# First expert layer of a fused two-layer kernel: a space of its own for every quad's weights, and another order of the matmuls

## The reference, cut to what matters

```python
xn = _layernorm(x)
x = x + _L0_attn_ref(xn, ...) + _L0_ffn_ref(xn, ...)   # causal attention, 8 heads; mixture of 14 experts
xn = _layernorm(x)
x = x + _L1_attn_ref(xn, ...) + _L1_ffn_ref(xn, ...)   # selective scan, 16 states; 8 experts, 2 per row

def _L0_ffn_ref(h, router_w, w1, b1, w2, b2):
    logits = x @ router_w
    assignments = jnp.argmax(logits, axis=-1)
    probs = jax.nn.softmax(logits, axis=-1)
    weights = jnp.take_along_axis(probs, assignments[:, None], axis=1)[:, 0]
    hid = jax.nn.gelu(jnp.einsum('nd,edf->nef', x, w1) + b1, approximate=False)
    all_out = jnp.einsum('nef,efd->ned', hid, w2) + b2
    sel = jnp.take_along_axis(all_out, assignments[:, None, None], axis=1)[:, 0, :]
    return sel * weights[:, None]
```

## Time and profile before

| what | value |
|---|---|
| time, median of 3 runs | 797.71 us (796.41 to 802.4) |
| the profiled execution's own time | 792.92 us |
| its span in the profile | 791.0 us |
| TensorE busy | 669.5 us, 85% |
| VectorE busy | 542.7 us, 69% |
| ScalarE busy | 400.5 us, 51% |
| the expert stage in the trace | 240.4 to 279.0 us |

### The profile page before, as it was taken

How to read it: one execution, slowest core, us unless ns; L and a number is a source line. 1 busy time by engine, 2 the same in 40 slices (tenths; PEclk the granted TensorE clock), 3 DMA queues, 4 the chain that set the end, 5 groups by cost and what they waited for, 6 DMA issues and landing times. The chain is left out here.

```text
span 791.0 us, 11454 instructions
## 1 busy us (share of the span) xinstructions
PE 669.5 (85%) x3446; PEld 462.2 (58%) x3447; DVE 542.7 (69%) x846; ACT 400.5 (51%) x810; POOL 227.0 (29%) x179
## 2 busy tenths in 40 slices
PE   3889999999989907879899998997787999977664
PEld 2666777777758804345566555554637988862222
DVE  6184444444332222499999999999794678997998
ACT  1246565655524503846765566555556566662330
POOL 0012122112200051002022212224036136668881
PEclk9589999999998966899999999999898999997998
DMA  8400000000336920214666767677734455521112
GB/s 287 147 3 11 11 11 10 7 7 7 113 120 192 313 63 17 63 54 116 164 165 157 182 150 174 148 182 184 238 77 131 146 177 159 172 69 37 27 33 60
DMA packets 59803, 86.74 MB, mean 110 GB/s; under 512 B 7505, under 2 KB 35922, under 8 KB 59762
## 3 DMA queue, kind: packets, MB, share of 16 engines
q1 hardware_dynamic: 41330, 57.89, 23.2%
q0 software_dynamic: 7680, 23.08, 13.5%
q10 hardware_dynamic: 10752, 5.24, 2.2%
HBM read 54.60 MB, written 14.81 MB: 88 GB/s over the span
## 5 line engine op out<-in xcount | busy, mean ns | idle before, releaser
L1538 DVE TENSOR_REDUCE nmax<-PS 128x1 f32<-128x128 f32 (+7 forms) x128 | 95.8, 748 | 90.3 <-PE PS L979 90.2
L1007 PE MATMUL PS<-ROOM 128*128 128x512 f32 (+3 forms) x384 | 142.5, 489 | 0.5 <-ACT ROOM L661 0.5
L668 ACT ACTIVATE ROOM<-PS,nmax 128x128 f32<-128x128 f32 (+7 forms) x128 | 95.7, 748 | 76.8 <-DVE nmax L1538 75.0
L661 ACT COPY ROOM<-PS 128x512 f32<-128x512 f32 (+1 forms) x192 | 85.8, 484 | 77.1 <-PE PS L991 76.9
L991 PE MATMUL PS<-CST,ROOM 128*128 128x128 f32 x576 | 85.7, 276 | 10.5 <-ACT ROOM L661 10.5
L542 POOL DMA_DIRECT2D ROOM<-ROOM x32 | 28.6, 893 | 214.9 <-DVE ROOM L1622 212.8
L991 PEld LDWEIGHTS PS<-CST,ROOM 128*128 128x128 f32 x576 | 64.3, 142 | 38.6 <-issue 28.1
L976 PE MATMUL PS<-LATER 128*128 128x512 f32 (+2 forms) x192 | 77.1, 511 | 8.1 <-ACT ROOM L668 5.8
L1007 PEld LDWEIGHTS PS<-ROOM 128*128 128x128 f32 x384 | 64.9, 191 | 28.3 <-issue 25.1
L1614 DVE TENSOR_TENSOR_SCAN ROOM<-ROOM 128x1024 f32<-128x1024 f32 x32 | 72.7, 2271 | 0.5 <-ACT ROOM L700 0.2
L507 POOL DMA_INDIRECT rows_in<-XN,slot x48 | 62.8, 1309 | 20.0 <-issue 12.4
(11 more groups left out here) (176 smaller groups left out, 1230.4 us busy)
## 6 DMA issues: line engine op xcount, KB each, us to landing
ROOM<-bc_rows SPq DMA_DIRECT2D x32, 512.0 KB, 4.1
ROOM<-ROOM POOLq DMA_DIRECT2D x32, 512.0 KB, 6.1
LATER<-in_w SPq DMA_DIRECT2D x48, 256.0 KB, 3.0
ROOM<-in_w SPq DMA_DIRECT2D x32, 321.0 KB, 3.9
rows_in<-zero SPq DMA_DIRECT2D x20, 256.0 KB, 3.2
LATER<-rows_in SPq DMA_DIRECT2D x24, 128.0 KB, 2.8
rows_out<-ROOM ACTq DMA_DIRECT2D x24, 128.0 KB, 2.0
ROOM<-rows_in SPq DMA_DIRECT2D x8, 256.0 KB, 4.1
```

The source lines that it names most:

```text
L661: nc.scalar.copy(dst, src).then_inc(s_ed, 1)
L668: nc.scalar.activation(PR[:, s, 0:nk], sc[:, 0:nk], ACT.Exp, bias=nmax[:, i % 4:i % 4 + 1], accum_out=rsum[:, i:i + 1]).then_inc(s_ex, 1)
L1007: r = mm(PS[:, 6, lo:BANK], V[:, j, :], PT[:, 4 * group + j, lo:BANK], start=j == 0, stop=True, skip_group_check=True)
L1538: nc.vector.tensor_reduce(nmax[:, i % 4:i % 4 + 1], sc[:, 0:(i + 1) * P], AX_X, ALU.max, negate=True).then_inc(s_nm, 1)
```

## The change

It gives every quad its own space for weights. Six of the eight are loaded as soon as the experts of the tiles are known and the queue gets there, which is during the first attention; the spaces of quads 6 and 7 still lie over `PT`. The GELU's results have two sets of buffers (`MH2`), and the hidden units' PSUM banks are 2 and 3 for even quads and 5 and 6 for odd ones. The loops of one pass are written out. The order on TensorE becomes turn(p), hidden(p), result(p-1). VectorE's order stays as it was.

```diff
-        W4 = (mw0[:, 0:4, :], mw0[:, 4:8, :], more_w, more_w2)
-        X4 = (MX[:, 0:4, :], MX[:, 4:8, :], more_x, more_x2)
+        quad_w = 4 * W_ROW[0]
+        W8 = [room(HEAD_END + i * quad_w, [4, W_ROW[0]]) for i in range(6)]
+        W8 += [room(29 * KB + i * quad_w, [4, W_ROW[0]]) for i in range(2)]
+        moe_at = HEAD_END + 6 * quad_w
+        MXT = room(moe_at, [8, P])
+        MH2 = (room(moe_at + 4 * KB, [8, P]), room(16 * KB, [8, P]))
+        MY = room(moe_at + 8 * KB, [8, D])
+        X4 = [room(moe_at + (12 + 2 * i) * KB, [4, D]) for i in range(3)] + [room(50 * KB, [4, D])]
...
+        HIDDEN_BANK = (2, 5)
...
             def first_expert_loads():
                 e_n = MOE[0][0]
                 sp.wait_ge(s_eid, 1)
+
+                def rows(p):
+                    if p >= 4:
+                        sp.wait_ge(s_mtp[0], p - 3)
+                    sp.dma_start(X4[p % 4], xs[0][p * 4 * P:(p + 1) * 4 * P, :].rearrange("(i p) d -> p i d", p=P)
+                                 ).then_inc(s_mx[0][p % 4], 16)
+
+                def weights(p):
+                    for i in range(4):
+                        e = sp.value_load(eid[0][0:1, 4 * p + i:4 * p + i + 1], min_val=0, max_val=e_n - 1)
+                        sp.dma_start(W8[p][:, i, :], A["w_0"][bass.ds(e, 1)].rearrange("o p n -> (o p) n")
+                                     ).then_inc(s_mw[p % 4], 16)
+
+                for p in range(6):
+                    weights(p)
                 sp.wait_ge(s_sc[0], 16 * NT)
...
+                for p in range(3):
+                    rows(p)
+                sp.wait_ge(s_we, 2 * HEADS)
+                rows(3)
+                weights(6)
+                weights(7)
+                for p in range(4, QUADS):
+                    rows(p)
...
                 turn_rows(0, 0, 1, True)
                 hidden(0, 0, 1)
                 turn_rows(1, 1, 1, True)
-                result(0, 0, True)
+                pe.wait_ge(s_ke, 4)
+                pe.wait_ge(s_ve, 4)
                 hidden(1, 1, 1)
-                for s in (2, 3):
-                    turn_rows(s, s, 1)
-                    result(s - 1, s - 1)
-                    hidden(s, s, 1)
-                with pe.Fori(1, QUADS // 4) as r:
-                    for s in range(4):
-                        turn_rows(4 * r + s, s, r + 1)
-                        result(4 * r + s - 1, (s - 1) % 4)
-                        hidden(4 * r + s, s, r + 1)
-                result(QUADS - 1, 3)
+                result(0, True)
+                for p in range(2, QUADS):
+                    turn_rows(p, p % 4, p // 4 + 1)
+                    hidden(p, p % 4, p // 4 + 1)
+                    result(p - 1)
+                result(QUADS - 1)
                 pe.wait_ge(s_my[0], QUADS)
...
             experts_first()
-            pe.wait_ge(s_ke, 4)
-            pe.wait_ge(s_ve, 4)
             transposes(2)
```

More of the change, by code:

```diff
@@ L133, in build @@
         KB = 256
-        HEAD_END, MOE_END, END = 53 * KB, 90 * KB, 133 * KB
+        HEAD_END, END = 53 * KB, 133 * KB
         ROOM = sb("ROOM", [P, END])
@@ L427, in first_expert_loads @@
                 sp.wait_ge(s_eid, 1)
-                sp.wait_ge(s_sc[0], 16 * NT)
[L430 to L443, removed]
-                for s in range(4):
[L446 to L449, removed]
+                def rows(p):
[10 more added lines that the diff above has]
+                    weights(p)
+                sp.wait_ge(s_sc[0], 16 * NT)
+                for p in range(3):
[6 more added lines that the diff above has]
+                    rows(p)
             def second_expert_loads():
@@ L726, in experts_first, with quad @@
             def experts_first():
-                def quad(p, s):
+                def quad(p):
                     for i in range(4):
@@ L731, in quad @@
                                 act.wait_ge(s_mhp[0], 2 * p + i // 2 + 1)
-                            w = W4[s][:, i, 4 * P:4 * P + 2]
-                            r = nc.scalar.activation(MH[:, 2 * i + c, :], PS[:, 2 + i // 2, (2 * (i % 2) + c) * P:(2 * (i % 2) + c + 1) * P],
+                            w = W8[p][:, i, 4 * P:4 * P + 2]
+                            r = nc.scalar.activation(MH2[p % 2][:, 2 * i + c, :], PS[:, HIDDEN_BANK[p % 2] + i // 2, (2 * (i % 2) + c) * P:(2 * (i % 2) + c + 1) * P],
                                                      ACT.Gelu, bias=w[:, c:c + 1])
@@ L740, in store @@
                                   ).then_inc(s_mo[0][s], 16)
[L743 to L750, removed]
+                quad(0)
+                for p in range(1, QUADS):
+                    quad(p)
+                    store(p - 1, (p - 1) % 2)
                 store(QUADS - 1, 1)
@@ L1114, in hidden, with result @@
                         for c in range(2):
-                            r = mm(PS[:, 2 + i // 2, (2 * (i % 2) + c) * P:(2 * (i % 2) + c + 1) * P],
-                                   W4[s][:, i, c * P:(c + 1) * P], MXT[:, 4 * (s % 2) + i, :], start=True, stop=True)
+                            r = mm(PS[:, HIDDEN_BANK[p % 2] + i // 2, (2 * (i % 2) + c) * P:(2 * (i % 2) + c + 1) * P],
+                                   W8[p][:, i, c * P:(c + 1) * P], MXT[:, 4 * (s % 2) + i, :], start=True, stop=True)
                         if i % 2:
                             r.then_inc(s_mhp[0], 1)
-                def result(p, s, first=False):
+                def result(p, first=False):
                     if not first:
@@ L1656, in rows, with result @@
                     cp(MXT[:, 4 * s:4 * s + 4, :], bank(s).rearrange("p (i n) -> p i n", n=P)).then_inc(s_mt[0], 1)
-                def result(p, w, s, times):
+                def result(p, s, times):
                     dve.wait_ge(s_myp[0], p + 1)
@@ L1663, in result @@
                     tt(MY[:, 4 * s:4 * s + 4, :], bank(4).rearrange("p (i n) -> p i n", n=P),
-                       W4[w][:, :, 4 * P + 2:4 * P + 2 + D], ALU.add).then_inc(s_my[0], 1)
+                       W8[p][:, :, 4 * P + 2:4 * P + 2 + D], ALU.add).then_inc(s_my[0], 1)
                 rows(0, 0)
[L1667 to L1682, removed]
+                for p in range(1, QUADS):
+                    rows(p, p % 2)
+                    result(p - 1, (p - 1) % 2, (p - 1) // 2 if p > 2 else None)
+                result(QUADS - 1, 1, QUADS // 2 - 1)
             def combine_first(b):
```

13 lines of the change are left out of this document (1 added, 12 removed).

## The result

The changed kernel took 809.6 us (median of 6 runs, 802.18 to 812.13) beside 799.57 us for the kernel before (6 runs, 791.17 to 803.47, the three of the table above among them). The ratio is 1.0135, 95% interval 1.0092 to 1.0178. Ratios here are of fast runs alone, without those more than 1.5% above the fastest of their kernel (here the 803.47), and so they are not the quotients of the medians. I had forecast +7.0 us, 0.9%, as a change within one per cent. It is slower by more than that in this comparison: 0.0135 of 797.71 is 10.8 us, and the two medians differ by 10.0. The time itself lies inside the range that I gave, 801.5 to 810.

The account below looks back on a forecast made before the run. TensorE was taken to bound the expert stage's steady quads, at 4.01 us each. Added 1.05 + 7.3 + 1.05 = 9.4 us, less 2.4 removed, gave +7.0 on 797.71: 804.7 us, 0.9% more, range 801.5 to 810.

Parts of the forecast that it names:

- Where the stage stands: Expert stage before GpSimd's first gather: it is exposed, so a microsecond there is a microsecond of the kernel.
- The waits for weights: TensorE's waits for late weights at quads 6 and 7 go: 2.09 us removed.
- The GELU: Between hidden and result: it never holds result up in steady quads, so two sets of its buffers bring nothing.
- the 0.3 us at the end: From quad 7's hidden to the last addition: 0.29 us read as waits for the last GELU, to be removed.
- The uncovered copy: Between turn and hidden: VectorE's copy of turned rows leaves gaps of 1.22 us in quads 2 to 7, 1.05 in quad 1.
- The end: Before the last result group: it waits 1.05 us for the addition of quad 6, as both results use bank 4.
- The sum: Whole expert stage: 9.4 us added less 2.4 removed, +7.0 us.
- The loads beside the attention: 24 weight transfers during the first attention, from about 155 to 179 us: cost zero, bounds zero to +2 us.
- The clock: TensorE in the expert stage: granted clock from 246 to 285 us not under 0.95, else the prediction is wrong.
- a rival with 14%: Expert stage: TensorE's clock falls one to three times among the gaps, 2.6 to 7.8 us more, about 809; chance 14%.
- How the numbers follow: Last step, whole kernel: forecast 76%, 22 points above the one per cent line; within 1% 0.58, slower 0.40, faster 0.02.

Follow-up runs that it names:

- e2: The changed kernel with the old order on TensorE (turn, result, hidden), all else of the change kept; 796.1 us beside 797.55, ratio 0.9993.
- e5: The changed kernel with VectorE's copy of quad p+1 put ahead of its addition of quad p-1; one run, 805.26 us.
- e6: The changed kernel with the results in PSUM banks 4 and 7 by turns; one run, 805.35 us.
- e1: The changed kernel measured again without edit; 805.63 us beside 797.55 for the kernel before, ratio 1.0098.
- e3: The changed kernel with all weight transfers moved back behind the wait for the scatters; 804.26 us beside 797.55, ratio 1.0087.
- e7: The changed kernel with four useless matmuls per quad between turn and hidden of quads 1 to 7; 804.63 us beside 799.82, ratio 1.0076.
- e10: The changed kernel measured a third time without edit; 813.4 us beside 806.25 for the kernel before, ratio 1.0080.

## Why the prediction was right in its sum and wrong in its call

- *Where the stage stands.* Right: from the last addition on everything moved with it, with 0.12 us more to the gather.
- *The waits for weights.* Right: gone, 2.08 us by e2 against 2.09.
- *The GELU.* Right: no quad waits for it, and the 0.3 us at the end belongs to the old order (e2).
- *The uncovered copy.* Right: 1.21 against 1.22, and both of its parts by e5: 1.05 for the trip over VectorE, and the rest for the addition in its way.
- *The end.* Right: 1.05 us, and e6 takes it away.
- *The sum.* +7.0 for the stage. Apart from the first, the traces of this order (e1, e3, e7, e10) had stages of 44.61 to 45.53 us against 44.93. Five comparisons of kernels with this order have ratios of 1.0135, 1.0098, 1.0080, 1.0087 and 1.0076; 7.0 us is 1.0088.
- *The loads beside the attention.* Right at zero: 0.2 us in the first trace, nothing that shows over all of them. The queue took 25.9 us to issue the 24, not 24.4, and was done at 181.5 to 184.6 and not at 179, still long before the scatters.
- *The clock.* Wrong by my own mark. I had asked for a granted clock of at least 0.95 from 246 to 285; it was 0.84 there in the first trace, 0.50 until 258.
- **The term of the sum that failed is the clock at the stage's start.** The sum took the start of the stage over from the one trace of the kernel before, as if the clock came back at the same time, and left a later return to a rival with 14%. Against the 44.93 of the sum the three traces of the changed kernel had +2.5, -0.15 and +0.6 us, and where more was needed it was the clock's late return after turn of quad 0. Their mean is 45.9, 7.9 above the mean of the two traces of the kernel before; the three comparisons together have 7.7, and the sum had 7.0. The rival priced this well, 2.6 us for one fall, but as a new fall among the gaps. What came was a late return from a fall ahead of the stage, which e2, with the old order, showed too, by 1 us. I count it to the spread of the executions, which is not shown.
- **The step that turned this into a wrong call is the last one, "How the numbers follow".** The forecast stood 1.0 us below the line of one per cent, and I called it "within 1%" with 0.58, with 22 of its 76 points above the line. The 7 us come on top of a time that differs by some 10 us from run to run, so a measurement could fall on either side of the line. The microsecond that the clock adds on the mean of the three traces would have put the sum at the line itself, and the chances at even. The direction was never in doubt, and on which side of the line a comparison fell was in part chance: of the three, two are below it.

Of the 3.8 us that the first comparison had beyond the sum, the clock's 2.5 is seen in one execution alone. The rest was not found in any cause, and the two later comparisons of the same kernel don't have it.

It stays open whether the new order costs up to 1 us more than its gaps, which the times of this kernel can't tell, and what sets the clock in the stretches before the stage, which no experiment varied.

## What to carry to other kernels

When an order of groups on TensorE is changed, write down for each group who has to touch its output before the next group may start: a group with a round trip over VectorE (here 1.05 to 1.22 us) needs another group between it and its reader. Doubling buffers for an engine that is never late (here the GELU) brings nothing by itself, and the order that it allowed cost 7 us, while one more quad of lead for the transposes and a second bank for the results turned the same buffers and early loads into a gain of 3. Before reading a difference of two traces, cut both at common marks: here nearly half of it lay in code that was the same. And take the spread of such a term as the clock's return from more than one trace before it goes into a sum.

## What I had not expected of the hardware

- In two of the three traces of the changed kernel (the first and e1) the pairs of L933 took 0.80 us from 19 us on, to the end of the pairs at 29. In the kernel before, such pairs took 0.80 where the granted clock was 0.50 (25 to 30 us) and 0.49 where it was 1.00 (15 to 20 us), but in these two traces the record of the granted clock shows 1.00 from 0 to 50 us. A record of 1.00 is worth holding against the durations of the same matmuls in another trace.
- The clock can be granted anew at different times in executions of one program: the changed kernel's hidden group of quad 1 took 3.49 us in one trace and 1.86 in the two others.
- The kernel's medians differ by 8.7 us between comparisons (797.55 to 806.25), and its time from the first gather to the end by 11.6 us (509.0 and 520.6), while its expert stage repeats to 0.2 us (37.89 and 38.06).
